# First attention's projections, suffix and three pairs of maxima in other softmax units of a transformer row

## The reference

```python
xn = layernorm(x)                       # x: 8 rows (batches) of 512 x 128, fp32
# s: attention 1 (16 heads of 8), causal, on xn
pressure = where(causal, -10000, q @ k.T * 8 ** -0.5)
attn = 1 - tanh((pressure - threshold) / tau) ** 2
s = (attn / (sum(attn) + 1e-6) @ v) @ Wo.T
# g: block 2 on xn
h = rmsnorm(xn);  X = xn + softmax(q2 @ k2.T * 8 ** -0.5) @ v2 @ wo
h2 = rmsnorm(X);  combine = softmax of the top 2 of softmax(h2 @ router)
g = silu(X + shared(h2) + sum_e combine[e] * expert_e(h2))    # swiglu, 8 experts, d_ff 256
out = x + s * g
```

## Time and profile before

| what | us |
|---|---|
| median of 3 runs | 1096.43 |
| lowest, highest | 1095.84, 1101.96 |
| profiled execution, its own time | 1097.14 |
| its span in the trace | 1095.4 |
| busy: TensorE, VectorE, ScalarE, GpSimd | 990.9, 831.4, 646.8, 351.2 |

### The profile page before, as it was taken

How to read it: one execution, slowest core, us unless ns; L and a number is a source line. 1 busy time by engine, 2 the same in 40 slices (tenths; PEclk the granted TensorE clock), 3 DMA queues, 4 the chain that set the end, 5 groups by cost and what they waited for, 6 DMA issues and landing times.

```text
span 1095.4 us, 18252 instructions
## 1 busy us (share of the span) xinstructions
PE 990.9 (90%) x6763; PEld 467.3 (43%) x6784; DVE 831.4 (76%) x1684; ACT 646.8 (59%) x882; POOL 351.2 (32%) x211
## 2 busy tenths in 40 slices
PE   4489999899998999889998999989999899988997
PEld 1123464245542455324652346523554245532464
DVE  6885977869776888759878598795977779773962
ACT  3569724786258842698336972379624785258731
POOL 4702443033520355105530154203352033610032
PEclk9589999999999999999999999999999999999999
DMA  7350561023700435105331055211471033600020
GB/s 231 71 109 22 111 169 34 21 55 80 190 20 12 99 93 132 30 2 130 112 83 30 2 130 143 51 31 30 101 181 24 21 79 83 163 20 2 1 79 10
DMA packets 60392, 81.83 MB, mean 75 GB/s; under 512 B 8560, under 2 KB 47728, under 8 KB 57296
## 3 DMA queue, kind: packets, MB, share of 16 engines
q1 hardware_dynamic: 56544, 75.61, 28.3%
q10 hardware_dynamic: 3760, 5.05, 1.4%
HBM read 52.98 MB, written 27.39 MB: 73 GB/s over the span
## 4 chain that ended last, share of the span: by engine, by line
PE 53%; DVE 25%; ACT 12%; issue 4%; DMA 2%; SPq 1%; ACTq 0%; POOL 0%; DVEq 0%; POOLq 0%
PE O L1156 11%; DVE nmax L758 10%; DVE PT L813 9%; PE O L1139 7%; ACT PT L613 7%; PE S L1172 6%; PE S L1174 5%; PE S L1173 5%; PE S L1112 4%; PE M L1075 3%; PE M L1054 2%; PE M L1080 1%; PE O L1075 1%; SPq L368 1%; DMA stackQ<-mTZ 1%
## 5 line engine op out<-in xcount | busy, mean ns | idle before, releaser
L613 ACT ACTIVATE PT<-S 128x1024 f32<-128x1024 f32 (+1 forms) x448 | 417.0, 967 | 113.7 <-PE S L1112 108.7
L813 DVE SCALAR_TENSOR_TENSOR PT<-PT 128x768 f32<-128x768 f32 (+1 forms) x192 | 213.4, 1163 | 101.0 <-ACT PT L613 101.0
L758 DVE TENSOR_REDUCE nmax<-M 128x1 f32<-128x512 f32 x329 | 218.2, 684 | 43.2 <-PE M L1075 28.3
L1139 PE MATMUL O<-PT,V 128*32 128x256 f32 (+3 forms) x2816 | 246.5, 430 | 0.0
L494 POOL TENSOR_TENSOR PT<-PT,CB 128x1024 f32<-128x1024 f32 x56 | 133.6, 2392 | 261.2 <-DVE PT L951 146.9
L646 ACT ACTIVATE PT<-S 128x1024 f32<-128x1024 f32 x72 | 73.9, 1027 | 241.4 <-PE S L1174 241.4
L479 POOL TENSOR_TENSOR split<-split,parts 128x512 f32<-128x512 f32 x30 | 90.9, 3029 | 372.0 <-ACT parts L573 372.0
L1112 PE MATMUL S<-stackQ,stackK 64*128 64x512 bf16 (+3 forms) x1024 | 166.3, 347 | 9.5 <-DMA stackQ<-mTZ 5.3
L758 DVE TENSOR_REDUCE nmax<-O 128x1 f32<-128x512 f32 x183 | 125.1, 684 | 36.5 <-PE O L1075 17.6
L1172 PE MATMUL S<-h2hi,wgu_hi 128*128 128x512 f32 x288 | 148.7, 516 | 4.3 <-DVE PT L951 4.2
L1156 PE MATMUL O<-PT,wdn 128*128 128x512 f32 x288 | 142.9, 595 | 0.9
(11 more groups left out here) (198 smaller groups left out, 1044.5 us busy)
## 6 DMA issues: line engine op xcount, KB each, us to landing
CB<-scrC SPq DMA_DIRECT2D x64, 256.0 KB, 5.6
stackQ<-scrQ SPq DMA_DIRECT2D x30, 384.0 KB, 5.5
stackK<-scrK SPq DMA_DIRECT2D x30, 384.0 KB, 6.3
scrQ<-parts SPq DMA_DIRECT2D x32, 192.0 KB, 3.3
scrK<-parts SPq DMA_DIRECT2D x30, 192.0 KB, 5.9
scrQ<-parts SPq DMA_DIRECT2D x32, 128.0 KB, 3.4
scrK<-parts SPq DMA_DIRECT2D x30, 128.0 KB, 5.2
KX<-scrK SPq DMA_DIRECT2D x14, 192.0 KB, 3.4
```

The lines of the kernel that those rows point to most:

```text
L613: a.activation(PT[:, n % SLOTS, 2 * q * w:2 * q * w + 2 * w].rearrange("p (r n) -> p r n", r=2), S[k][:, :].rearrange("p (r n) -> p r n", ...
L758: v.tensor_reduce(nmax[:, h % 2, h // 2, t:t + 1], M[k][:, :], AX.X, ALU.max, negate=True).then_inc(m_read[k], 1)
L813: v.scalar_tensor_tensor(p, p, 1.0, p, ALU.subtract, ALU.mult).then_inc(weighed, 1)
L1139: last = t_.matmul(O[k][32 * q:32 * q + VW, i0:i1], V[:, j, 4 * g + q, :], PT[:, n % SLOTS, w * q + at:w * q + at + i1 - i0], start=(j == ...
```

## The change

Q1, K1 and V1 of a row are computed in its own units 2, 4 and 6 and its suffix in unit 9, behind `maxT_Z`. The maxima of Y and Z move: three pairs at the passage instead of one and one behind it, and the last pair of Z ends in unit 8 as its only one. `maxT_Y` comes at the head of unit 5. Q1, K1 and V1 may use the third bank. On SP Q1's stores come ahead of Y's rows, Q1's load and K1's stores behind them, K1's load behind Z's rows. On GpSimd the splits of Q1 and K1 stand between the copy to x1 and V1's sums. On VectorE `out_by_s` comes behind six maxima, `out_gated` behind eight. `corr` gets a tile of its own. In the start the same work falls away.

```diff
-spread(MAX["Y"], {0: 2, 1: 2, 2: 4, 3: 4, 4: 4})
-spread(MAX["Z"], {5: 4, 6: 4, 7: 4, 8: 4})
+spread(MAX["Y"], {0: 4, 1: 2, 2: 4, 3: 4, 4: 2})
+spread(MAX["Z"], {4: 2, 5: 4, 6: 4, 7: 4, 8: 2})
 PLACES[3].insert(2, "outT")
-PLACES[5].insert(2, "maxT_Y")
-PLACES[9] += ["maxT_Z"]
+PLACES[5].insert(0, "maxT_Y")
+PLACES[9] += ["maxT_Z", "suffix"]
+for n, name in ((2, "Q1"), (4, "K1"), (6, "V1")):
+    PLACES[n].append(name)
...
-PLACES[25] += ["Q1"]
 PLACES[26] += ["h2T"]
-PLACES[27] += ["logits", "K1"]
-PLACES[EXPERT] += ["suffix"]
...
-PLACES[EXPERT + 4].insert(2, "V1")
-PLACES[EXPERT + 4].insert(4, "ctxT1")
+PLACES[EXPERT + 4].insert(3, "ctxT1")
...
+THREE = {"Q1", "K1", "V1"}
+AHEAD = {"xnT", "hT", "Q2", "K2", "V2", "maxT_X", *MAX["X"], "maxT_W", *MAX["W"]}
...
-            k = min(range(3 if name[0] == "max" else 2), key=lambda b: last[b])
+            k = min(range(3 if name[0] == "max" or name in THREE else 2), key=lambda b: last[b])
...
-        corr = h2T[:, :].rearrange("p (t d) -> p t d", t=NT)
+        corr = sb("corr", [128, NT, D])
...
-                    for k in range(2):
-                        wait_apart(sp, s_full[k], it * S_USES + UNITS)
                     spread_weights(u, it)
-                    restack("Q1", 2, bt)
-                    restack("K1", 3, bt)
...
-                for run in ("Y", "Z"):
-                    wait_apart(sp, *read(u, "maxT_" + run))
-                    maxima_rows(run)
+                store_parts("Q1", 2, it)
+                wait_apart(sp, *read(u, "maxT_Y"))
+                maxima_rows("Y")
+                if it == 0:
+                    sp.wait_ge(setup, 2)
+                    sp.wait_ge(kset, 4)
+                load_stack(sp, "Q1", it)
+                store_parts("K1", 3, it)
+                wait_apart(sp, *read(u, "maxT_Z"))
+                maxima_rows("Z")
+                load_stack(sp, "K1", it)
...
-                wait_apart(pool, *read(ROWS[it - 1] if it else FIRST, "V1"))
+                for name in ("Q1", "K1"):
+                    for _step in split_steps(u, name, it, True):
+                        pass
+                wait_apart(pool, *read(u, "V1"))
...
-                    if following and e < 3:
-                        for _step in split_steps(u, ("Q1", "K1")[e - 1], it + 1, True):
-                            pass
...
-                    for name in u.places[n]:
+                    for i, name in enumerate(u.places[n]):
+                        if n == 2 and i == 2 and it > 0:
+                            out_gated(it - 1)
                         take(u, it, name)
-                    if it == 0 and n == 10:
-                        constants()
-                    if n == 0 and it > 0:
+                    if n == 1 and it > 0:
                         out_by_s(it - 1)
-                    if n == 1 and it > 0:
-                        out_gated(it - 1)
...
-                        take(u, it, "suffix")
...
+                if k == 2:
+                    pe.wait_ge(o_read[1], it * O_USES[1] + 1)
...
+            def seam_maxima(it, n, i):
+
+                for name in ROWS[it].places[n][i:i + 2]:
+                    work(ROWS[it], it, name)
+
             def row(u, it, following):
                 v_at = {n: n - 2 for n in range(2, N1 + 2)} | {n: n - 3 for n in range(N1 + 3, UNITS)}
-                for name in u.places[1]:
...
-                for _step in second_product(it, NE - 2):
-                    pass
+                for f, _step in enumerate(second_product(it, NE - 2)):
+                    if following and f == 0:
+                        work(u, it, "maxT_W")
+                        seam_maxima(it + 1, 0, 0)
                 if following:
-                    work(u, it, "maxT_W")
                     for q in range(2):
                         scores(it + 1, 1, q)
-                    for name in ROWS[it + 1].places[0]:
-                        work(ROWS[it + 1], it + 1, name)
+                    seam_maxima(it + 1, 0, 2)
                 for t in range(NT):
                     last = t_.matmul(O[0][:, t * 128:t * 128 + 128], x1[:, t, :], ident[:, :], start=False, stop=False)
                 last.then_inc(down_done, 1)
+                if following:
+                    seam_maxima(it + 1, 1, 0)
```

More of the change, by code:

```diff
@@ L83 @@
 PLACES[23] += ["proj2"]
-PLACES[25] += ["Q1"]
 PLACES[26] += ["h2T"]
-PLACES[27] += ["logits", "K1"]
-PLACES[EXPERT] += ["suffix"]
+PLACES[27] += ["logits"]
 PLACES[EXPERT + 1] += [("oT1", 0), "combT"]
@@ L359, in restack @@
                     store_part(sp, name, i, part)
+            def restack(name, i, bt):
+                store_parts(name, i, bt)
                 load_stack(sp, name, bt)
@@ L393, in prepare @@
                     maxima_rows(run)
[L394 to L403, removed]
             def spread_weights(u, it):
@@ L499, in row @@
                 g.tensor_scalar(x1[:, :, :], xn[:, :, :], 1.0, None, ALU.mult).then_inc(carried, 1)
-                wait_apart(pool, *read(ROWS[it - 1] if it else FIRST, "V1"))
+                for name in ("Q1", "K1"):
+                    for _step in split_steps(u, name, it, True):
+                        pass
+                wait_apart(pool, *read(u, "V1"))
                 if it > 0:
-                    wait_apart(pool, *full(ROWS[it - 1] if it else FIRST, "suffix"))
+                    wait_apart(pool, *full(ROWS[it - 1], "suffix"))
                 g.tensor_tensor(VS[:, 1, :], V1c[:, 2, :], V1c[:, 3, :], ALU.add).then_inc(v_summed, 1)
@@ L524, in _ @@
                 last.then_inc(pv_done, SLOTS // 2)
-            for name in ("Q1", "K1"):
-                for _step in split_steps(FIRST, name, 0, False):
-                    pass
             for it in range(B):
@@ L566, in projection @@
                 scale = {"Q2": {"scale": HD ** -0.5}, "Q1": {"scale": qs1[:, :]}}.get(name, {})
+                if name == "Q1":
+                    act.wait_ge(scaled, 1)
                 if i >= 2:
@@ L594, in take @@
                 elif name in ("Q2", "K2", "Q1", "K1"):
-                    projection(u, name, bt)
+                    projection(u, name, bt if name[1] == "2" else bt - 1)
             def acc_out(it, P):
@@ L667, in _ @@
                 for name in FIRST.places[n]:
-                    if name == "Q1":
-                        act.wait_ge(scaled, 1)
-                    if name in ("V2", "V1"):
-                        act.wait_ge(v_set, 1 if name == "V2" else 2)
+                    if name == "V2":
+                        act.wait_ge(v_set, 1)
                     if name != "maxT_W":
@@ L918, in row @@
                             maxima_parts(u, run)
+                    if it == 0 and n == 8:
+                        constants()
                 if following:
@@ L1214, in work @@
                     if name == "Q1":
-                        wait_read(u, "xnT", name)
+                        pe.wait_ge(*read(ROWS[it - 1] if it else FIRST, "xnT"))
                     w, src = (w2s, hT) if name[1] == "2" else (w1s, xnT)
-                    projected(u, name, w[:, 0 if name[0] == "Q" else 1, :], src)
+                    projected(u, it, name, w[:, 0 if name[0] == "Q" else 1, :], src)
                 elif name in ("V2", "V1"):
-                    projected_v(u, name, (w2s if name == "V2" else w1s)[:, 2, :], hT if name == "V2" else xnT)
+                    projected_v(u, it, name, (w2s if name == "V2" else w1s)[:, 2, :], hT if name == "V2" else xnT)
                 elif name[0] in ("oT2", "oT1"):
@@ L1275, in first_scores @@
                     scores(it, 0, q)
+            def seam_maxima(it, n, i):
+                for name in ROWS[it].places[n][i:i + 2]:
+                    work(ROWS[it], it, name)
             def row(u, it, following):
                 v_at = {n: n - 2 for n in range(2, N1 + 2)} | {n: n - 3 for n in range(N1 + 3, UNITS)}
-                for name in u.places[1]:
-                    work(u, it, name)
                 for n in range(2, UNITS):
@@ L1343, in _ @@
                 scores(0, 1, q)
-            for name in ROWS[0].places[0]:
-                work(ROWS[0], 0, name)
+            for n, i in ((0, 0), (0, 2), (1, 0)):
+                seam_maxima(0, n, i)
             for it in range(B):
```

21 lines of the change are left out of this document (10 added, 11 removed).

## The result

The changed kernel takes 1113.25 us in the median of four runs (1111.13 to 1113.54), the kernel before 1097.27 beside it (1095.84 to 1101.96). The ratio is 1.013 (95% interval 1.0113 to 1.0146): slower by 1.3%. The forecast of 1089.0 has the wrong sign, and the time lies outside its range. The profiled execution took 1111.13 us, the fastest of the four; the other three took 1113.2 to 1113.5, at a mean granted clock of 0.967 instead of its 0.970. What follows splits up this fastest one.

The account below looks back on a forecast made before the run. Limits: TensorE in the experts, VectorE in units 2 to 9 and second attention, ScalarE in units 10 to 15. Six middle rows -7.6 (-2.56 + 1.3 each), row 0 -0.6, row 7 +0.7: total -7.5, so 1089 us; range 1077 to 1103.

Parts of the forecast that it names:

- The experts: Expert stage: suffix and GpSimd's split leaving the router's chain gives -1.75 us, V1 leaving -0.81; -2.56 in rows 0 to 6.
- GpSimd's contention: Router in the experts: without Q1's split beside it, VectorE's stretch was to take 1.15 us less.
- The second attention: Q1, K1 and their activations leave; costed at nothing beyond the 1.13 already used, gain up to 0.4 us possible.
- Units 10 to 15: After units 2 to 9: ScalarE sets the pace, so the earlier delay stays; no extra cost was given.
- Units 2 to 9: VectorE starts 1.7 us ahead, TensorE gains four pieces of work; between 0 and +4.5 us, taken as +1.3 including the passage.
- The passage: From experts to next row: two more maxima pairs ahead of the last down product, 2 x 0.33 = 0.66 us later.
- Row 7: Last row: +1.3 us, with only the suffix's 0.6 gained at the experts; +0.7 in all.
- The start and row 0: Start 0, its chain not passing Q1, K1, V1; row 0 +2.0 - 2.56 = -0.6 us.
- Rival 2: Y's rows queue behind Q1's stores on SP and reach unit 8 3.0 us late: 1113 us; chance 0.12.
- rival 3: Experts gain only V1, as the row's tail hides the rest: 1101 us; chance 0.13.
- Rival 1: Units 2 to 9: idle time of VectorE and TensorE hides everything, +0 instead of +1.3: 1079 us; chance 0.20.
- Rival 4: VectorE's casts wait on GpSimd's Q1 and K1 splits, 1.2 us per row, depending on 0.5 us of order: 1098; chance 0.10.

Follow-up runs that it names:

- The two fillers: Changed kernel plus two 512-column matmuls per row, at h2T and the logits, whose results nothing reads: 1104.81 us, ratio 1.0074.
- the thinned kernel: Kernel before with Q1's and K1's matmuls of the next row cut to 32 of 512 columns: 1097.71 us, ratio 0.9996.
- the swapped copy: Changed kernel with two filling matmuls, ScalarE copying maxT_W between unit 0's two exponentials instead of behind them: 1102.92 us, ratio 1.0036.
- the last experiment: Changed kernel with two filling matmuls, Q1's and K1's matmuls and ScalarE's copies of them cut to 32 of 512 columns: 1109.3 us, timed once.

## Why the prediction failed, step by step

**The experts held.** -1.76 and -0.88 against -1.75 and -0.81. One thing in the reasoning was too simple. I booked 1.15 us for GpSimd's contention as if it were a gain by itself; taken away alone it gives nothing, as TensorE arrives at the same moment. It counts only with TensorE's 2.61 us freed, which the prediction did require ("TensorE must be there in time").

**"The second attention: I cost this at nothing; a loss I see no cause for"** is the step that failed most. 6.95 us of the 13.87 come from it, in the profiled execution; the other three lost 2 to 2.4 us more, at a lower mean clock. I asked what covers the work that leaves, and found VectorE; I did not ask what TensorE does in the gap. Q1 and K1 were what kept TensorE's gaps there short. The two fillers take the falls away, and the thinned kernel has them. So TensorE's missing work there is shown as a cause in kind. It is not the whole of it; how often it strikes (two long falls and a short one here, a long and a short one in the thinned kernel, one short one in the kernel without its passage, which has as little work there and the same two rests) is not explained.

**Units 10 to 15 "keep ScalarE's pace, so the delay stays".** The suffix was inside the 22.8 us of TensorE's sum for units 2 to 9, to be over before unit 10, and no price was put on it behind mhZ. It stands behind Z's turning, where VectorE has no maxima left and ScalarE paces with no slack: 1.61 us, all of it bare. Two kernels with the suffix in different places show the same (-1.48 and +1.76).

**Units 2 to 9, VectorE's head start of 1.7.** It is there: 2.02 us in the kernel with the passage alone. The three projections then eat it but for 0.13 us. They take 3.2 us of TensorE, and 1.89 of it show on the way to mhZ. Q1's and K1's matmuls account for 0.69, the copies by themselves for 0.28; what V1 and the banks have of the rest was not tried. From sT to mhZ I expected 19 to 21 us, and it was 22.15.

**The passage, "2 x 0.33 = 0.66".** It cost 1.84. The missing term is a bank: I counted the maxima's own time, and not that the first pair now stands behind `maxT_W`, whose bank ScalarE frees only after two exponentials, 0.83 us. Shown by the swapped copy (-0.47). The remaining 0.35 is not taken apart.

Together units 2 to 15 and the passage are 1.84 - 0.13 + 1.61 = +3.32 us a row against the +1.3 forecast; with -2.64 of the experts that is the +0.68 (measured +0.66 at full clock) where -1.26 was forecast.

Row 7's +0.85 is near the forecast of +0.7 by luck: there units 2 to 15 cost 1.48 us, with no passage behind them, and the forecast had 1.3 with one.

**The start and row 0, forecast 0 and -0.6**, measured +2.65. The clock comes up to full about 2 us later (63.5 instead of 61.8), and Q1 runs at half clock, 2.1 us at 61.60. That isn't all: with ScalarE's copies cut the clock is full at 61.7, and the first sT is still at 189.59, 1.8 us late; and the kernel with the passage alone starts 3.6 us later. No run or row shows the forecast's +2.0 for row 0 by itself, and the start's loss was not isolated.

**The rivals.** Rival 2 (Y's rows late) did not occur, nor rival 3. Rival 1's hope that idle time hides everything failed by the bank and the suffix. Rival 4 was absent in the changed kernel and present in the last experiment, so its 0.5 us of order was the right thing to look at. In the changed kernel mhY stood 1.4 us ahead of K1's split, forecast 0.7. The time came from none of the rivals.

## What to carry to other kernels

Work moved off an engine that is not the limit can still cost, if it was what kept TensorE's clock up: look at the gaps that stay behind, and at the granted clock of that stretch in several executions. In a stretch paced by one engine, ask how far ahead the other is, not how busy it is: ScalarE was the limit in units 10 to 15, and TensorE had almost nothing in hand. A moved matmul also takes over the bank and its reader, so price the wait for the reader's place in its own queue. And a contention taken away is worth only as much as the next chain allows: where two chains are tied, take both.

## What the runs showed of the hardware that I had not expected

TensorE's clock fell from 1.00 to 0.50 (1.2 GHz) behind two gaps of 1.31 and 0.86 us, with TensorE busy 3.69 and 4.14 of 5 us, and stayed low for about 10 us, nearly all of them dense work; the same load in another row of the same execution left it at 1.00. The price was 3.15 to 3.3 us for each of these two falls. In the last experiment three falls came in units 2 to 9.

A cast of 16 columns by VectorE took 1.04 us instead of 0.16 when a GpSimd operation of 1.15 us had started 0.14 us before it. The Trainium skill's page SBUF — State Buffer (section SBUF: two separate sides) says that whoever starts first has the shared ports for the whole instruction. This trace agrees. The page names VectorE operations with two SBUF inputs or in a two-port mode; this cast has one input, so by the page it would have run in a two-port mode, which no run here shows.
